# The opening of a routed feed-forward: own semaphore for the first weights, second weights from GpSimd's queue, constant rows from SyncE and ScalarE

## The reference, cut to what matters

```python
logits = t @ switch_w + switch_b            # t: 2048 x 128, 8 experts
route_prob_max = jnp.max(softmax(logits), -1)
routes = jnp.argmax(route_prob, -1)
for e in range(8):                          # w1[e]: 128 x 512, w2[e]: 512 x 128
    y = gelu(t @ w1[e] + b1[e]) @ w2[e] + b2[e]
    out = jnp.where((routes == e)[:, None], y, out)
x = x + 0.5 * out * route_prob_max[:, None]
```

## Time and profile before

| what | us |
|---|---|
| runs | 750.75, 757.09, 755.23 |
| median | 755.23 |
| span of the profiled execution | 752.3 |
| TensorE busy | 581.5 (77%) |
| VectorE busy | 532.0 (71%) |
| ScalarE busy | 453.5 (60%) |
| GpSimd busy | 203.6 (27%) |

### The profile page before, as it was taken

The page is one execution under the profiler, slowest core; times in us unless marked ns, Lnnn a source line. Parts: engine busy times, 40 slices in busy tenths (PEclk is TensorE's granted clock), DMA queues, the critical chain, the costliest instruction groups (busy, mean ns, idle before and its releaser), DMA issues. The chain is left out here.

```text
span 752.3 us, 17249 instructions
## 1 busy us (share of the span) xinstructions
PE 581.5 (77%) x5361; PEld 417.1 (55%) x5361; DVE 532.0 (71%) x1881; ACT 453.5 (60%) x983; POOL 203.6 (27%) x262
## 2 busy tenths in 40 slices
PE   4399993079999999999899998452996673678780
PEld 3288883045666666767576766341985342346450
DVE  7543320967787788999799995873224799867897
ACT  3245562047888888999799996550552534376723
POOL 1745332401912720660400000043443200211200
PEclk9999998589999999999999999655998787799985
DMA  8878567699899999999744421833554000000001
GB/s 241 221 240 289 181 215 205 212 300 331 242 349 330 296 313 309 255 251 345 185 136 141 134 65 22 238 86 127 170 180 121 2 1 0 0 1 1 1 1 56
DMA packets 130378, 127.80 MB, mean 170 GB/s; under 512 B 27962, under 2 KB 108002, under 8 KB 129394
## 3 DMA queue, kind: packets, MB, share of 16 engines
q1 hardware_dynamic: 122722, 99.85, 46.7%
q0 software_dynamic: 3920, 25.26, 8.8%
q10 hardware_dynamic: 3648, 1.59, 0.8%
HBM read 68.37 MB, written 48.79 MB: 156 GB/s over the span
## 5 line engine op out<-in xcount | busy, mean ns | idle before, releaser
L1714 DVE CUSTOM_DVE_ANT_0 l0am_prob<-l0am_ps_s,l0am_bias 128x512 f32<-128x512 f32 x256 | 166.6, 689 | 33.8 <-PE l0am_ps_s L1788 24.1
L1631 ACT ACTIVATE l0am_prob<-l0am_prob,l0am_neg_top 128x512 f32<-128x512 f32 x256 | 171.4, 723 | 6.8 <-DVE l0am_neg_top L1714 6.8
L1801 PE MATMUL l0am_ps_t<-c_ident,l0am_prob 128*128 128x128 f32 x1024 | 129.0, 275 | 0.4 <-DVE l0am_probT L1701 0.4
L1801 PEld LDWEIGHTS l0am_ps_t<-c_ident,l0am_prob 128*128 128x128 f32 x1024 | 110.9, 141 | 16.5 <-issue 8.0
L636 ACT ACTIVATE l0f_h<-l0f_psU,l0f_experts 128x128 f32<-128x128 f32 x212 | 60.7, 369 | 83.0 <-PE l0f_psU L962 82.9
L829 DVE COPY l0f_xsT<-l0f_psT 128x128 f32<-128x128 f32 x53 | 15.4, 291 | 99.0 <-PE l0f_psT L952 99.0
L1701 DVE COPY l0am_probT<-l0am_ps_t 128x512 f32<-128x512 f32 x128 | 82.2, 684 | 1.4 <-PE l0am_ps_t L1801 1.4
L1788 PE MATMUL l0am_ps_s<-l0am_ks,l0am_qs 32*128 32x512 f32 x512 | 74.4, 651 | 3.5 <-DVE l0am_neg_top L1714 2.6
L1625 ACT COPY l0am_probT<-l0am_ps_t 128x512 f32<-128x512 f32 x128 | 68.5, 589 | 10.7 <-PE l0am_ps_t L1801 10.7
L531 POOL DMA_INDIRECT token_results<-l0f_ys,l0f_token_i x53 | 51.1, 965 | 78.3 <-DVE l0f_ys L839 75.0
L1815 PE MATMUL l0am_ps_cg<-l0am_probT,l0am_v 128*9 128x128 f32 x2048 | 68.7, 275 | 2.7 <-DVE l0a_heads L1725 2.7
(11 more groups left out here) (340 smaller groups left out, 949.6 us busy)
## 6 DMA issues: line engine op xcount, KB each, us to landing
l0am_bias<-near_terms SPq DMA_DIRECT2D x128, 192.0 KB, 4.6
near_terms<-l0am_near POOLq DMA_DIRECT2D x6, 3072.0 KB, 12.3
l0f_mine<-l0f_experts SPq DMA_DIRECT2D x53, 256.0 KB, 2.4
near_terms<-l0am_near SPq DMA_DIRECT2D x4, 1536.0 KB, 7.5
l0o_rows_k<-position_k SPq DMA_DIRECT2D x12, 512.0 KB, 6.9
l0f_experts<-in_L_ffn_w SPq DMA_DIRECT2D x2, 2048.0 KB
l0f_experts<-in_L_ffn_w SPq DMA_DIRECT2D x16, 256.0 KB
position_q<-l0o_rows SPq DMA_DIRECT2D x16, 256.0 KB, 4.3
```

The costliest lines, as they stand in the source:

```text
L1631: nc.scalar.activation(prob[:, k, :], prob[:, k, :], ACT.Exp, bias=neg_top[:, k:k + 1], scale=-1.0)\
L1714: dve.tensor_tensor_reduce(out=prob[:, k, :], in0=ps_s[:, j, :], in1=bias[:, j, at:at + S], scale=-1.0, scalar=HUGE, op0=ALU.add, op1=ALU.min,
L1801: last = pe.transpose(ps_t[:, BANK_OF[j], i, :], prob[:, u % SLOTS_, i * P:(i + 1) * P], ident[:, :])
```

## The change

In both feed-forwards the first weights count on a semaphore of their own, `up_weights_in`, the second on `down_weights_in`, and b1 and b2 on `weights_in`; SyncE waits for the first weights and `rows_ready` and no longer for `b1_ready`, and TensorE waits for the other two before it turns b1. In the first feed-forward alone, GpSimd issues the eight second-weight DMAs, ahead of its scatters; SyncE stores the first four blanks of the first part and all eight of the second part, and ScalarE the other four of the first part.

```diff
-FFN_LOADS = 3 + EXPERTS
...
+        EARLY_BLANKS = 4 if opening else 0
+        LATER_BLANKS = range(2, 2 + EXPERTS)
...
+        def load_down_weights(queue):
+            for e in range(EXPERTS):
+                queue.dma_start(experts[:, e, SLAB_W2:SLAB_B2].rearrange("p (k d) -> p k d", k=FC),
+                                w["w2"][e].rearrange("(k p) d -> p k d", p=P)).then_inc(down_weights_in, 16)
+        def store_blank(queue, part, e, stored):
+            end = queue.value_load(blank_i[0:1, part, e:e + 1], min_val=0, max_val=XS_ROWS - P)
+            queue.dma_start(xs_dram[bass.ds(end, P), :], c["blank"][:, e, 0:XS_COLS]).then_inc(stored, 16)
...
-                sp.wait_ge(weights_in, FFN_LOADS * 16)
-                sp.wait_ge(b1_ready, 1)
+                if opening:
+                    sp.wait_ge(blanks_ready, 1)
+                    for e in range(EARLY_BLANKS):
+                        store_blank(sp, 0, e, blanked[e])
+                sp.wait_ge(up_weights_in, 16)
                 sp.wait_ge(rows_ready, 1)
...
                         row = packed_of(sp, s + AHEAD)
+                        if opening and s in LATER_BLANKS:
+                            if s == LATER_BLANKS[0]:
+                                sp.wait_ge(blanks_ready, 2)
+                            e = LATER_BLANKS.index(s)
+                            store_blank(sp, 1, e, later_blanked[e])
                         load_mine(s + AHEAD, row)
                         load_tokens(s + AHEAD, row)
...
                 pool.wait_ge(ids_set, 1)
+                if opening:
+                    load_down_weights(pool)
...
-                    if opening and s < EXPERTS:
-                        if s == 0:
-                            pool.wait_ge(blanks_ready, 2)
-                        pool.indirect_dma_start(
-                            xs_dram[:, :], bass.IndirectOffsetOnAxis(ap=blank_i[:, 1, s:s + 1], axis=0),
-                            c["blank"][:, s, 0:XS_COLS], None).then_inc(later_blanked[s], 16)
...
-                for e in range(EXPERTS):
-                    end = act.value_load(blank_i[0:1, 0, e:e + 1], min_val=0, max_val=XS_ROWS - P)
-                    act.dma_start(xs_dram[bass.ds(end, P), :], c["blank"][:, e, 0:XS_COLS]).then_inc(blanked[e], 16)
+                for e in range(EARLY_BLANKS, EXPERTS):
+                    store_blank(act, 0, e, blanked[e])
...
-                pe.wait_ge(weights_in, FFN_LOADS * 16)
+                pe.wait_ge(weights_in, 2 * 16)
+                pe.wait_ge(down_weights_in, EXPERTS * 16)
```

More of the change, by code:

```diff
@@ L400, in ps_rank @@
             return psU[:, g % 2, 0, 0:5 * EXPERTS].rearrange("p (t e) -> p t e", t=5)
-        weights_in = sem("weights_in")
+        weights_in, up_weights_in = sem("weights_in"), sem("up_weights_in")
+        down_weights_in = soft_dma_sem("down_weights_in")
         chain = sem("chain")
@@ L411, in ffn_phase @@
         blanked = [sem(f"blanked{e}") for e in range(EXPERTS)]
-        later_blanked = [soft_dma_sem(f"later_blanked{e}") for e in range(EXPERTS)] if opening else []
+        later_blanked = [sem(f"later_blanked{e}") for e in range(EXPERTS)] if opening else []
         b1_psum, b1_ready = sem("b1_psum"), sem("b1_ready")
@@ L445, in _ @@
             def _(sp):
[L446 to L452, removed]
-                for e in range(EXPERTS):
-                    sp.dma_start(experts[:, e, SLAB_W2:SLAB_B2].rearrange("p (k d) -> p k d", k=FC),
-                                 w["w2"][e].rearrange("(k p) d -> p k d", p=P)).then_inc(weights_in, 16)
+                sp.dma_start(b1[:, :], w["b1"].rearrange("e (k p) -> (e k) p", p=P)).then_inc(weights_in, 16)
+                sp.dma_start(experts[:, :, SLAB_W1:SLAB_W2], w["w1"].rearrange("e d f -> d e f")).then_inc(up_weights_in, 16)
+                sp.dma_start(experts[:, :, SLAB_B2:SLAB_B1], w["b2"].unsqueeze(0).partition_broadcast(P)).then_inc(weights_in, 16)
+                if not opening:
+                    load_down_weights(sp)
                 if aside:
```

## The result

The changed kernel took 761.6 us (median of 9 runs, 757.3 to 765.0); the kernel before, timed beside it, 753.1 us (9 runs). The ratio is 1.0104, with a 95% interval of 1.0075 to 1.0133: 8 us slower, or 1.0%. The forecast was 759.3 us (754 to 765), from a kernel before at 755.2. As a change it was +4.1 us; measured are +8.5 by the medians and +9.0 by the spans. The profiled execution has a span of 761.3 us against 752.3.

A forecast was written before the change was run, and what follows sets the result against it. SyncE's unbroken issue list was taken to bound the first feed-forward. Opening -5.5, blanks +10.0 and a vanished wait -0.4 gave +4.1 us: span 752.3 to 756.4, plus 2.9 makes 759.3 us, range 754.0 to 765.0.

The forecast's parts named there:

- the likeliest case: First feed-forward: SyncE's list starts 5.5 us earlier and pays 10.0 us for blanks; +4.1 us, 759.3 us; chance 0.60.
- the second rival: Opening: GpSimd's weight loads held past 18.4 us, or SyncE's own start held; +8.1 us, 763.3 us; chance 0.18.
- the opening's gain: Opening of the first feed-forward: SyncE goes on at 25.2 instead of 30.72 us, gaining 5.5 us (bounds 5.9 and -0.8).
- The rule to read by: First feed-forward: it ends when SyncE has issued its list; additions are paid one for one while SyncE stays last.
- The blanks: eight make 10.0 us: SyncE's list, slots 6 to 13: eight added stores at 1.25 us each cost 10.0 us (bounds 2.9 and 16.2).
- The first rival: SyncE has unseen slack, so the phase moves with TensorE's first turn, -3.1 us, to 752.1 us; chance 0.12.
- the upper bound: Opening: SyncE's small loads held until 22.1 us as before, its blanks then ending at 31.5, eating the gain.
- What starts the list earlier is gained: First feed-forward: an earlier start of SyncE's list ends the phase earlier by as much, while SyncE stays last.
- The 0.4 us that SyncE waited for ScalarE goes: SyncE's list in the first feed-forward: this wait vanishes because SyncE comes later; -0.4 us.
- TensorE at most some 4.5 us late, ends near 125: First feed-forward: from slot 13 TensorE is delayed by SyncE's rows at most some 4.5 us, still ending ahead of SyncE.
- SyncE's last table load near 134: End of the first feed-forward: a sign that the forecast is right, SyncE's last table load ending near 134 us.
- GpSimd's weight loads: Opening: eight second-weight loads take 8.9 us from about 5, done near 14, hidden ahead of the first scatter near 18.4.

The follow-up runs named there:

- run 1: Changed kernel with the eight second-part blanks stored by GpSimd again, behind its result scatters; opening's change kept: 753.08 us, ratio 1.0004.
- run 2: Kernel before with only the eight second-part blanks moved from GpSimd to SyncE's loop: 761.88 us, ratio 1.0118.
- experiment 3: Changed kernel with four of the eight second-part blanks on SyncE and the other four on GpSimd: 758.52 us, ratio 1.0056.
- run 4: Changed kernel with GpSimd's eight second-weight loads issued behind its fourth token scatter: 759.84 us, ratio 1.0066.
- run 5: Kernel before with a semaphore of their own for the first weights, SyncE waiting for that one only; loads and blanks unmoved: 752.5 us, ratio 0.9967.
- run 6: Changed kernel with all blanks off SyncE, eight on ScalarE and eight on GpSimd; only the weights' part kept: 753.12 us, ratio 1.0015.
- Run 8: Kernel of experiment 7 with TensorE's wait for the second weights moved to its first down product: 750.67 us, ratio 0.9931.
- experiment 10: Changed kernel with two groups of table loads moved from SyncE's tail to ScalarE, timed twice: 761.24 us, ratio 1.0103; 758.29 us, ratio 1.0085.
- experiment 7: Changed kernel with second-part blanks on GpSimd and GpSimd's second-weight loads behind its fourth token scatter: 752.14 us, ratio 0.9979.
- experiment 9: Kernel of Run 8 with two groups of table loads moved from SyncE's tail to ScalarE: 750.11 us, ratio 0.9937.

## Why the prediction was right, and where it was not

The forecast named the loss, its side and its place, and was 2.3 us short in time, but only half of the change was in it: +4.1 us where +8.5 to +9.6 came. That the time still lies near it is in part luck. Its base was 755.2, the median of three runs; nine runs put that kernel at 753.1. And the 2.9 us that it added to the span compare three runs with another execution: in the recorded runs the time is 1.7 to 2.1 us above the run's own span. The mechanism was that of the likeliest case, the size that of the second rival (0.18), whose sum of +8.1 has the opening's gain at 1.5. The ratio of 1.0104 lies just past the line of 1% that the forecast gave a chance of 0.19. By its own steps:

- **"The rule to read by: what is put on the list is paid, one for one".** Right for this change (runs 1 to 3). SyncE's last load moved by 9.6 us and the phase by 9.6 us. Against before, SyncE was 1.3 us early at slot 5, 9.0 late at slot 13, 10.2 late at slot 29 and 9.6 late at its last load.
- **"The blanks: eight make 10.0 us".** Right: 10.3 us between slots 5 and 13, 1.29 each against 1.25; 9.4 us at the phase's end in run 2, 9.3 from run 1 to the changed kernel. The Trainium skill's rule that issuing "is usually small relative to the DMA itself" (DMA: Bandwidth & Descriptors, issuing engines are not separate DMA queues) does not decide here: the store's DMA instruction takes 0.36 us, but its whole place in the list 1.29, and a queue that issues without a break pays all of it. The first rival, which rested on that, is out.
- **"The opening: I take 25.2, a gain of 5.5".** This is the step that failed, by the size of one term. It measured 1.45 us at the first copy. I argued that "the small loads need room only behind one weight DMA"; in truth the first of them was held until 21.11, close to the 22.1 that I had set as the upper bound. The bound was right, the point in it wrong: I compared bytes in SyncE's queue and left out that GpSimd's 2 MB would move through the same 16 engines at the same time (run 4: 6.05 us of hold without them). The Trainium skill (DMA: Bandwidth & Descriptors, queues, rings and completion order) has the rule I should have weighed: an engine takes turns between the queues that have work for it, a packet at a time. The rows of the queues agree in that q0 and q1 progressed side by side, 1.90 and 2.75 MB; how the turns went they do not show.
- **"What starts the list earlier is gained".** This failed too, and with it the whole opening. Runs 5 and 6 start SyncE 3.9 and 5.2 us earlier than before and end the phase no earlier: waits for ScalarE's blanks (3.3 and 3.1 us) take the place of the wait removed, and the rest goes along the list. Run 8 starts 7.2 us earlier and keeps 2.9. Each of these is one trace against one, so that a gain of up to 1.5 us would not show.
- **"The 0.4 us that SyncE waited for ScalarE goes".** It did not go. SyncE came 10 us later and still waited 0.8:

```profile
SPq L1304 <- ACT l0o_rows L1298: 0.8, 1, 0.8
```

- **"TensorE at most some 4.5 us late, ends near 125".** 125.36 is right by luck. The step took TensorE's delay to be SyncE's at slot 13, which was 9.0 and not 4.5; TensorE's turn that waited at 68.73 before came at 74.03, 5.3 late, so the step was wrong in what it equated. Its first turn came at 37.44, not near 34. **"SyncE's last table load near 134"** was 139.81, by the opening's missing 4 us, by another 1.2 us that SyncE lost from slot 13 to 29, and by the wait that did not go.
- **GpSimd's weight loads:** 6.24 us instead of 8.9, done at 11.51, as forecast hidden. The delay of a cast beside a scatter is not a rule of this trace: two more casts of that line began inside scatters, at 25.38 and 28.76, and took 0.18 us. The second rival blamed GpSimd's issuing; its price (+8.1, 763.3) was near the result, and of its two mechanisms it was the one given in half a sentence, the start held on SyncE itself, that came true.
- **Not foreseen:** the second bound, GpSimd's landing and drain. It does not enter the loss, but it is why taking work off SyncE soon stops paying: SyncE's end lay 1.6 us behind GpSimd's before and 5.4 in the changed kernel, where experiment 10 made 3.7 and 1.6 us of it at the phase's end.

## What to carry to other kernels

A store that is added to a queue which issues without a break costs its whole place in the list, register loads included, and costs nothing on an engine that waits for results anyway, as long as it comes in time there (it did in experiment 1 and did not in experiment 7). Moving a load to another engine's queue frees issue time but not the DMA engines: ask what its bytes will run beside, for the first weights can land later by it (18.6 us after their issue against 11.9 here). And before a wait at the head of a chain is removed, list what the waiting engine will ask for next, and when each of these lands; a gain at the start is worth only what the latest of them leaves.

## What the runs showed of the hardware

- SyncE's queue, with 2.5 MB of weights issued to it, held the next load, of 64 KB, for 6.05 us alone (and, in the kernel before, one of 256 KB for 5.79), and for 13.17 us with a software queue moving 1.90 MB beside it. The holding shows as the duration of the issuing instruction, not as a wait.
- GpSimd issued eight weight loads of 256 KB in 6.24 us (0.78 each) and they landed after a median of 10.3 us. SyncE had needed 13.63 us for the same eight behind its own backlog.
- GpSimd's drain at the end of the phase took 3.90 to 5.20 us in the 14 traces, and its length goes with the DMAs that GpSimd had issued in the phase: 47 and 3.90 us (experiment 2), 55 and 4.55 (before and changed, among others), 59 and 4.88 (experiment 3), 63 and 5.20 (experiments 1 and 6 to 9), some 0.08 us for each DMA. Why is not shown. It stands in no list of busy time; there it is idle time ahead of the next phase's first instruction, and only the view of its line shows it.
- The register load of a slot on SyncE, the same instruction each time, took 0.26 to 1.16 us in the kernel before. The profile shows no wait for it.
